# A graph-attention layer on one core: one product for K, V and Q rows, every gather from the K/V table, and gathers held closer to the compute

## The reference

```python
Q = x @ Wq + bq;  K = x @ Wk + bk;  V = x @ Wv + bv      # per node
E = edge_attr @ We + be                                  # per edge
score = (K[src] * Q[dst] / sqrt(12) * E).sum(-1)         # per edge and head
score = exp(clip(score, -5, 5))
wV = segment_sum(V[src] * score, dst);  Z = segment_sum(score, dst)
out = layernorm(x + wV / (Z + 1e-6))
```

## Time and profile before

| what | value |
|---|---|
| median of three runs | 1014.6 us |
| profiled execution, its span (the page shows no time around it) | 1301.3 us |
| POOL busy | 748.1 us (57%) |
| PE busy | 672.6 us (52%) |
| DVE busy | 653.2 us (50%) |
| ACT busy | 177.1 us (14%) |
| mean granted TensorE clock | 0.729 of full speed |

### The profile page before, as it was taken

How to read it: one execution, slowest core, us unless ns; L and a number is a source line. 1 busy time by engine, 2 the same in 40 slices (tenths; PEclk the granted TensorE clock), 3 DMA queues, 4 the chain that set the end, 5 groups by cost and what they waited for, 6 DMA issues and landing times.

```text
span 1301.3 us, 12054 instructions
## 1 busy us (share of the span) xinstructions
PE 672.6 (52%) x3352; PEld 461.0 (35%) x3352; DVE 653.2 (50%) x1307; ACT 177.1 (14%) x337; POOL 748.1 (57%) x788
## 2 busy tenths in 40 slices
PE   3834744755345464455564355545454565445343
PEld 3833422533223343333343233333333333333223
DVE  4311634864346554455554454555455555455446
ACT  1413101111011111011110111011011111111011
POOL 7172465265656665666666565666666666666640
PEclk8756866877677766767778676677767777677777
DMA  7643543544435444544545354544544445445420
GB/s 178 222 145 105 161 126 94 147 125 130 135 100 138 119 132 111 133 132 130 138 120 145 94 153 103 137 134 120 136 131 129 134 128 137 115 136 138 115 70 21
DMA packets 101206, 165.87 MB, mean 127 GB/s; under 512 B 45132, under 2 KB 63853, under 8 KB 101133
## 3 DMA queue, kind: packets, MB, share of 16 engines
q1 hardware_dynamic: 62829, 84.39, 23.4%
q0 software_dynamic: 37152, 75.74, 22.2%
q10 hardware_dynamic: 1152, 4.92, 0.9%
HBM read 152.57 MB, written 12.39 MB: 127 GB/s over the span
## 4 chain that ended last, share of the span: by engine, by line
another core or an unknown queue 40%; issue 22%; DVE 17%; PE 15%; ACT 4%; DMA 1%; DVEq 0%; SPq 0%
DVE qe L830 5%; PE psE L451 4%; DVE logit L919 4%; ACT qe L632 3%; PE psA L521 3%; PE psT L472 3%; DVE qke L910 2%; DVE clipped L925 1%; PE psQ L431 1%; DVE q_parts L809 1%; DVE ob L882 1%; PE psA L482 1%; DVE place L818 1%; DVE msg L937 1%
## 5 line engine op out<-in xcount | busy, mean ns | idle before, releaser
L390 POOL DMA_INDIRECT kv<-kv_table,idx x758 | 724.6, 956 | 514.3 <-issue 218.1
L521 PE MATMUL psA<-place,msg 128*104 128x104 f32 x1536 | 206.4, 301 | 339.7 <-DVE msg L937 253.5
L521 PEld LDWEIGHTS psA<-place,msg 128*104 128x104 f32 x1536 | 193.0, 212 | 369.9 <-DVE msg L937 270.5
L818 DVE TENSOR_TENSOR place<-psI,rel_tile 128x832 f32<-128x832 f32 (+1 forms) x99 | 98.6, 996 | 322.9 <-remote 322.9
L451 PE MATMUL psE<-ea,we 97*96 97x512 f32 x392 | 241.8, 750 | 0.8 <-ACT xt L613 0.8
L632 ACT ACTIVATE qe<-psE 96x1024 f32<-96x1024 f32 (+1 forms) x99 | 99.9, 1009 | 573.4 <-remote 432.5
L830 DVE TENSOR_TENSOR qe<-psQ,qe 96x1024 f32<-96x1024 f32 (+1 forms) x99 | 118.9, 1201 | 60.7 <-ACT qe L632 35.5
L472 PE MATMUL psT<-identity,qe 96*128 96x96 f32 x782 | 109.7, 297 | 74.5 <-DVE qe L830 56.2
L472 PEld LDWEIGHTS psT<-identity,qe 96*128 96x128 f32 x782 | 92.1, 174 | 88.9 <-DVE qe L830 63.8
L910 DVE TENSOR_TENSOR qke<-psT,kv 128x768 f32<-128x768 f32 (+1 forms) x99 | 92.9, 938 | 29.0 <-remote 25.1
L451 PEld LDWEIGHTS psE<-ea,we 97*96 97x96 f32 x392 | 71.5, 206 | 74.5 <-issue 73.5
(11 more groups left out here) (117 smaller groups left out, 405.6 us busy)
## 6 DMA issues: line engine op xcount, KB each, us to landing
ea<-eaT SPq DMA_DIRECT2D x99, 384.0 KB
q_parts<-rel_table SPq DMA_DIRECT2D x99, 252.0 KB
kv<-kv_table,idx POOLq DMA_INDIRECT x758
qwin<-q_table SPq DMA_DIRECT2D x198, 23.6 KB
xb<-xrows SPq DMA_DIRECT2D x24, 144.0 KB
out<-ob SPq DMA_DIRECT2D x24, 144.0 KB
q_table<-q_parts SPq DMA_DIRECT2D x4, 720.0 KB
kv_table<-kv ACTq DMA_DIRECT2D x2, 960.0 KB
```

The source lines that it names most:

```text
L390: pool.indirect_dma_start(kv[:, k, t], None, kv_table, sources).then_inc(kv_in[k], 16)
L521: last = nc.tensor.matmul(sums[0:ML, off:off + PW], msg[:, s, t], place[:, s, t], start=opens, stop=closes)
L818: nc.vector.tensor_tensor(place[:, k % 2, 0:nt], ps_ids.unsqueeze(1).broadcast_to([P, nt, PW]), rel_tile[:, bass.ds(g * T, nt)].unsqueeze( ...
```

## The change

The three groups that were gathered from the input go away, with their transposes, copies and products; all 99 groups gather from `kv_table`, and the first gather waits for `kv_out` and the whole of `idx`. K, V and Q rows come from one product of 288 columns; the banks are now three pairs (`node_banks`). ACT copies K and V to `kv_stage`, and Q, scaled, as float32 to a new tile `q_full` in SBUF. The split into parts reads `q_full`: ACT's leading parts are put between the copies, DVE's remainders are made in place (five of them ahead of the window tables, five behind), all ten middle parts come after all leading ones. `q_table` is stored in the eight chunks of `KV_CHUNKS`. The order of some loads on SP changes. `CLOSE` becomes 2, so the wait for `q_done` begins with group 2 instead of 16; and from group 2 on the second half of a group's gathers also waits for `t_done` of the group two back.

```diff
-CLOSE = 2 * U
+CLOSE = 2
-XG = 3
-Q_CHUNKS = (10, 10, 10, 10, 5, 5)
+EARLY_QUERIES = 5
-        xg = sb("xg", [P, XG, T, D], f32)
+        q_full = sb("q_full", [P, NR // P, D], f32)
-        kv_banks = [psE[:, 0], psE[:, 1], psA[:], psT[:, 0]]
+        node_banks = [psE, psQ, psT]
 # SP
-                        sp.dma_start(idx[:, 0:XG * T], src[:, 0:XG * T]).then_inc(idx_in, 16)
...
+                        sp.dma_start(idx[:], src).then_inc(idx_in, 16)
 # POOL
                         if first and at == 0:
                             pool.wait_ge(idx_in, 16)
-                        if first and at == XG:
-                            pool.wait_ge(idx_rest_in, 16)
                             pool.wait_ge(kv_out, 16 * len(KV_CHUNKS))
                         k = at % U
                         for t in range(tiles(at)):
+                            if first and at >= CLOSE and t == tiles(at) // 2:
+                                pool.wait_ge(t_done, at - 1)
                             sources = bass.IndirectOffsetOnAxis(ap=idx[:, at * T + t:at * T + t + 1], axis=0)
-                            if first and at < XG:
-                                pool.indirect_dma_start(xg[:, k, t], None, xrows, sources).then_inc(xg_in[k], 16)
-                            else:
-                                pool.indirect_dma_start(kv[:, k, t], None, kv_table, sources
-                                                        ).then_inc(kv_in[k], 16)
+                            pool.indirect_dma_start(kv[:, k, t], None, kv_table, sources).then_inc(kv_in[k], 16)
 # PE
-                                if n >= 4:
-                                    pe.wait_ge(kv_up, n - 3)
+                                if n >= 3:
+                                    pe.wait_ge(kv_up, n - 2)
+                                    pe.wait_ge(q_full_up, n - 2)
                                 for j in range(2):
-                                    last = nc.tensor.matmul(kv_banks[n % 4][:, j * 2 * D:(j + 1) * 2 * D],
-                                                            nodes[:, t + j], wn[:, 0:2 * D],
+                                    last = nc.tensor.matmul(node_banks[n % 3][:, j, 0:3 * D], nodes[:, t + j], wn[:],
                                                             start=True, stop=True)
-                        for tile, size in chunked(Q_CHUNKS):
...
-                        for n in range(2 * XG):
-                            pe.wait_ge(xg_in[n // 2], 16 * T)
...
-                        for g in range(XG):
-                            convert(g)
 # ACT
+                            nc.scalar.activation(kv_stage[:, 2 * n:2 * n + 2], node_banks[n % 3][:, :, 0:2 * D],
+                                                 ACT.Copy).then_inc(kv_up, 1)
+                            nc.scalar.activation(q_full[:, 2 * n:2 * n + 2], node_banks[n % 3][:, :, 2 * D:3 * D],
+                                                 ACT.Copy, scale=float(HD) ** -0.5).then_inc(q_full_up, 1)
                             if n in ends:
                                 store_nodes(n)
+                            if 2 * n >= QB * (split + 1):
+                                leading(split)
+                                split += 1
...
+                        for n in range(NR // P // QB):
+                            middle(n)
 # DVE
+                            nc.vector.tensor_tensor(q_full[:, n * QB:(n + 1) * QB], q_full[:, n * QB:(n + 1) * QB],
+                                                    q_parts[:, n * QB:(n + 1) * QB, 0], ALU.subtract).then_inc(q_r, 1)
```

More of the change, by code:

```diff
@@ L165, in gnn_program @@
         tables_chain, tables_up, rel_out = sem("tables_chain"), sem("tables_up"), sem("rel_out")
-        idx_in, idx_rest_in = sem("idx_in"), sem("idx_rest_in")
-        xg_in = [sem(f"xg_in{i}") for i in range(XG)]
-        turned, turned_up, conv_mm, conv_up = sem("turned"), sem("turned_up"), sem("conv_mm"), sem("conv_up")
+        idx_in = sem("idx_in")
         kv_in = [sem(f"kv_in{i}") for i in range(U)]
@@ L264, in _ @@
                         sp.wait_ge(xt_in[3], 16)
-                        load_nodes(5)
+                        for c in range(5, len(KV_CHUNKS)):
+                            load_nodes(c)
                         sp.wait_ge(range_up, 1)
@@ L282, in _ @@
                     if first:
-                        for c, (tile, size) in enumerate(chunked(Q_CHUNKS)):
+                        for c, (tile, size) in enumerate(chunked(KV_CHUNKS)):
                             if c == 0:
@@ L395, in _ @@
                     for s in range(U):
-                        groups = len(range(s, NG, U)) - (1 if first and s < XG else 0)
+                        groups = len(range(s, NG, U))
                         missing = (T - TAIL_TILES[s]) if s < len(TAIL_TILES) else 0
                         pool.wait_ge(kv_in[s], 16 * (T * groups - missing))
-                    if first:
-                        for s in range(XG):
-                            pool.wait_ge(xg_in[s], 16 * T)
                     nc.gpsimd.dma_reset()
@@ L415, in _ @@
                                 n = (tile + t) // 2
-                                if n >= 4:
-                                    pe.wait_ge(kv_up, n - 3)
+                                if n >= 3:
+                                    pe.wait_ge(kv_up, n - 2)
+                                    pe.wait_ge(q_full_up, n - 2)
                                 for j in range(2):
-                                    last = nc.tensor.matmul(kv_banks[n % 4][:, j * 2 * D:(j + 1) * 2 * D],
-                                                            nodes[:, t + j], wn[:, 0:2 * D],
+                                    last = nc.tensor.matmul(node_banks[n % 3][:, j, 0:3 * D], nodes[:, t + j], wn[:],
                                                             start=True, stop=True)
                                 last.then_inc(kv_mm, 1)
-                        pe.wait_ge(kv_up, NR // P // 2)
-                        for tile, size in chunked(Q_CHUNKS):
[L425 to L434, removed]
                         pe.wait_ge(we_in, 16)
                         pe.wait_ge(ones_set, 3)
-                        pe.wait_ge(q_r, NR // P // QB)
+                        pe.wait_ge(q_full_up, NR // P // 2)
                     def halves_of(at):
@@ L526, in _ @@
                         pe.wait_ge(ids_up, 2)
-                        for n in range(2 * XG):
-                            pe.wait_ge(xg_in[n // 2], 16 * T)
[L529 to L549, removed]
                     edge_rows(0, 0, 0)
-                    if first:
-                        for g in range(XG):
-                            convert(g)
                     query_rows(0, 0, 0)
-                    if first:
-                        pe.wait_ge(conv_up, T // 2 * XG)
                     to_rows(0, 0, 0)
@@ L581, in store_nodes, with leading, middle @@
                                 kv_stage[:, tile:tile + size]).then_inc(kv_out, 16)
+                        def leading(n):
+                            act.wait_ge(q_full_up, -(-QB * (n + 1) // 2))
+                            nc.scalar.activation(q_parts[:, n * QB:(n + 1) * QB, 0], q_full[:, n * QB:(n + 1) * QB],
+                                                 ACT.Copy).then_inc(q_hi, 1)
+                        def middle(n):
+                            act.wait_ge(q_r, n + 1)
+                            nc.scalar.activation(q_parts[:, n * QB:(n + 1) * QB, 1], q_full[:, n * QB:(n + 1) * QB],
+                                                 ACT.Copy).then_inc(q_mid, 1)
@@ L583, in _ @@
+                        split = 0
                         for n in range(NR // P // 2):
                             act.wait_ge(kv_mm, n + 1)
[L585 to L588, removed]
+                            nc.scalar.activation(kv_stage[:, 2 * n:2 * n + 2], node_banks[n % 3][:, :, 0:2 * D],
+                                                 ACT.Copy).then_inc(kv_up, 1)
+                            nc.scalar.activation(q_full[:, 2 * n:2 * n + 2], node_banks[n % 3][:, :, 2 * D:3 * D],
+                                                 ACT.Copy, scale=float(HD) ** -0.5).then_inc(q_full_up, 1)
@@ L610, in _ @@
-                    if first:
-                        for n in range(2 * XG):
-                            act.wait_ge(turned, n + 1)
-                            nc.scalar.activation(xt[0:D, n * 4 * P:(n + 1) * 4 * P], turn_banks[n % 4][0:D, :],
-                                                 ACT.Copy).then_inc(turned_up, 1)
+                        for n in range(split, NR // P // QB):
+                            leading(n)
+                        for n in range(NR // P // QB):
+                            middle(n)
@@ L655, in _ @@
                     edges_up(0, 0, 0)
-                    if first:
-                        act.wait_ge(kv_out, 16 * len(KV_CHUNKS))
```

(19 more changed lines are left out.)

44 lines of the change are left out of this document (7 added, 37 removed).

## The result

The changed kernel takes 1049.05 us (median of four runs, 1048.28 to 1050.42), the kernel before, timed beside it, 1015.25 us (1014.39 to 1017.43): a ratio of 1.0336, with a 95% interval of 1.032 to 1.0352. It is slower by 34 us. The forecast was 1052.6 us.

The account below looks back on a forecast made before the run. The prediction took POOL's chain of gathers, 1.25 us each, to bound the kernel. 1014.6 + 30.0 (lost lead) + 5 (later table) + 3 (query rows) = 1052.6 us, own range 1040 to 1070, widened to 1030 and 1078.

Parts of the forecast that it names:

- What bounds the kernel: Whole kernel: a chain of gathers on POOL, 1.25 us each, first table gather at 49.4 us, 18 us after the last.
- the stops: Halts of POOL, DVE and ACT about every two groups, some 12 us each, taken as belonging to the profiled execution only.
- half-group hold: Second half of a group's gathers waiting for `t_done`: covered at group 2 and, by 18 us, in the loop; costs nothing.
- The lead: Start of POOL: 24 gathers of the first three groups move behind the table, nothing hides them, +30.0 us.
- The table: Node phase: the 288-column product makes the K/V table later, +5 us, bounds -5 and +9.5.
- The query rows: Gathers from group 2 on wait for the first query rows: +3 us, bounds 0 and 11.
- DVE beside POOL: Early gathers lengthened by DVE's splits with both operands in SBUF: 0 to 5 us, taken as nothing.
- the rest of the node phase: Second product, transposes and conversions leave PE and ACT: nothing won, as POOL is still busy with its first eight groups.
- The stops are real: Rival: timed runs are also held every second group, so the change saves 29 us, giving 986 us; chance 0.09.
- The lead was partly wasted: Rival: POOL waits for first messages before its ninth group, losing some 5 us of lead: 1048 us; chance 0.08.
- The half-group hold binds: Rival: in the loop landing takes 18 us longer, POOL runs in step with PE, about 1150 us; chance 0.04.
- The lead is made up: Rival: the table comes 30 us earlier and the time stays as before; chance 0.04.

Follow-up runs that it names:

- e1: The kernel before, unchanged, profiled once more: 1015.02 us (one run), a span of 1013.3 us.
- e3: The changed kernel without the second half group's wait for `t_done`, the wait for query rows from group 2 on kept: 1050.16 us, ratio 1.0347.
- e5: The changed kernel, unchanged, timed once more in five rounds beside other variants: 1050.33 us, ratio 1.0353.
- e4: The kernel before with all groups gathered from the K/V table, both products and the old holds kept: 1044.85 us, ratio 1.0286.
- e6: The changed kernel with three groups gathered from the input again and without both holds, leaving the merged product alone: 1014.16 us, ratio 1.0009.
- e10: The changed kernel with every last part of the Q rows computed twice on DVE, once into an unread tile: 1048.63 us.
- e2: The changed kernel without the wait for `t_done` and with `CLOSE` back at 16: 1044.33 us, ratio 1.0285.
- e7: The kernel before with four groups gathered from the input instead of three (`XG` = 4): 1009.12 us, ratio 0.9951.
- e9: The changed kernel with four groups gathered from the input and without both holds, the merged product kept: 1006.08 us, ratio 0.9918.

## Why the prediction was right, step by step

**What bounds the kernel: right.** The chain on POOL, at 1.25 us a gather, sets the time before and after, and the stops belonged to one profiled execution. The first table gather of before was put at 49.4 us from the median; it is at 43.6 (e1), and the missing 6 us lie in the pace: 757 intervals at (995.27 - 43.56) / 757 = 1.257 us instead of 1.25 are 5.5 us. From the end of the last gather to the end of the span are 1013.3 - 996.2 = 17.1 us, where 18 had been taken.

**The sum, term by term,** by the two profiles without stops. The last gather starts at 1030.03 instead of 995.27, 34.8 us later:

| term | predicted | measured | from |
|---|---|---|---|
| 24 gathers more behind the table | +30.0 | +30.1 | 24 x 1.255 |
| the table later | +5 | -3.3 | 40.24 - 43.56 |
| up to the 17th gather | +3 | +9.8 | 70.11 - 40.24 - 16 x 1.255 |
| half-group hold | 0 | 0 | e3 against e5 |
| pace of the other gathers | 0 | -1.8 | 757 x (1.2548 - 1.2572) |

*The lead: right,* and it is 29 of the 34 us by the times too (e4).

*The table: wrong in its sign.* Two parts of the step failed. The first is the price of 96 more columns. At the faster of two paces, a pair of tiles of the changed kernel starts 0.97 us after the one before it (x4 is one pair):

```profile
28.73 1.13 PE L404 MATMUL psE<-wn,xt 97*128 97x288 f32 x4
29.70 1.13 PE L404 MATMUL psQ<-wn,xt 97*128 97x288 f32 x4
```

In e1 (x8 is two pairs) it is 0.92 us on the mean of the 17 pairs from 18.98 us on:

```profile
30.93 1.94 PE L419 MATMUL psE<-wn,xt 97*128 97x192 f32 x8
32.70 1.10 PE L419 MATMUL psA<-wn,xt 97*128 97x192 f32 x4
33.64 1.10 PE L419 MATMUL psT<-wn,xt 97*128 97x192 f32 x4
34.57 0.81 PE L419 MATMUL psE<-wn,xt 97*128 97x192 f32 x4
```

The granted clock is 1.00 in both stretches. So 96 columns more cost 0.05 us a pair there, not 0.19; what else sets the length of a pair, no run separates. The first few pairs of both runs go at a slower pace, and between 192 and 288 columns the price there is larger than the 0.38 us taken: 1.28 us a pair in e1, 1.92 in the changed kernel. The step had set a bank of the earlier trace rows against a pair of the earlier trace rows as if only columns differed.

The second part is "the chain runs over PE". The last K/V store is issued at 36.4 us in the changed kernel and at 36.0 in e1, so PE and ACT are done no earlier; but it lands 3.0 us after its issue instead of 6.9. The end of the table is set by the stores' way through DMA, which the step had only as its lower bound, -5 from the x rows' traffic. Without the lead e4 has -2.8 and the changed kernel -3.3; e6, with the lead back, has +0.3.

*The query rows: the mechanism right, its size too small.* They are there 30 us after the table, near the upper end of 31 and far from the 11 without a queue. From the last split (48.2 us) to the first window load are 15.4 us, where 5.5 had been taken from the earlier trace rows. For 11.4 of them SP waits for the stores of `q_table`. By the pages of the changed kernel and of e1, a store of 720 KB takes 9.5 us to land instead of 4.5 (what, number, size, us to landing), as the changed kernel issues its eight stores within 6 us and e1 its six over 17:

```profile
q_table<-q_parts SPq DMA_DIRECT2D x2, 720.0 KB, 9.5
...
q_table<-q_parts SPq DMA_DIRECT2D x4, 720.0 KB, 4.5
```

By the window below the DMA engines of the changed kernel are full meanwhile, at 0.91 of their time and 316 GB/s.

```profile
40.20:62.20 22.00, 3.70 (x4) 0.96 (x4) 8.03 (x15) 3.90 (x6) 17.39 (x16) 0.58 0.91 316
```

That the stores and not the splits set this time, e10 shows. The 5.5 us had been taken from a stretch without a gather, in which the DMA engines were busy for 0.35 of their time (115.40 to 120.90 us in the trace of before). Of the 9.8 us, 7.6 are the wait beyond the usual issue time and 2.2 the slower gathers ahead of it. Without the holds, 7 us are saved by the times (e2), less than 9.8, as the slow gathers stay.

*DVE beside POOL: in its bounds, hidden.* Five gathers took 1.25 to 1.56 us instead of 0.95, all beside splits, and e10 makes it eight: within 0 to 5 us, and covered by the wait. The traces show a hold until the split at hand is over: a gather that begins beside a single split ends 0.82 us after that split, at 66.60 after 65.78 in the earlier trace rows and at 54.84 after 54.02 in e1:

```profile
53.60 1.24 POOL L390 DMA_INDIRECT kv<-kv_table,idx  x1 [0.30 <-issue]
```

Beside splits that follow one another every 0.57 us, the gathers start 1.71 us apart, three splits, and each ended after 1.40 us, so POOL is not held until the row of DVE's steps is over. The Trainium skill ("SBUF — State Buffer", on the "DVE blocks DMA" trap) has GpSimd unable to write descriptors while certain DVE operations run, with an fp32 copy as its example. The traces agree with such a hold to the end of one operation, here for a subtract of two operands in SBUF.

*The half-group hold and the rest of the node phase: right,* zero each (e3, e6).

So +5 + 3 = +8 stood where -3.3 + 9.8 - 1.8 = +4.7 was measured; the -1.8 us of the pace no run explains. Two wrong sizes of opposite sign left 3.6 us between the forecast and the time; that it is so little is luck, and the 30 us are owed to the chain.

**The rivals.** *The stops are real:* fell with e1. *The lead was partly wasted:* fell for the kernel before, where POOL's waits for messages are 1.2 us in all, four times the usual issue time; with a lead of four it is real (e7, 5.4 us). *The half-group hold binds:* fell with e3. *The lead is made up:* the table would have had to come 30 us earlier; it came 3.3.

**What would show it.** "First gather between 45 and 65 us" was wrong: 40.2, by the sign of the table's term. 782 gathers at 1.25 us, the wait ahead of the 17th gather (number 16 from zero) that ends with the first query rows, and no long wait for `to_rows` came as said.

What caused the stops stays open. Two profiled executions of one kernel have spans of 1301.3 and 1013.3 us, and no run tells what released the engines in the first.

## What to carry to other kernels

Where one queue issues at a steady pace and never rests, a change is priced by when that queue starts and what it waits for, and work taken from other engines is worth nothing until the queue waits for it (e6 against e9). A hold on such a queue costs what is missing between its place in the queue and the event, so the same line cost 7 us in one kernel and 37 in another. Set a suspicious profile against the median of the timed runs before anything is built on its waits.

## What the runs showed of the hardware that was not expected

- A profiled execution was 288 us longer than another of the same kernel, with stops every two groups, while the timed runs differ by 3 us.
- At a granted clock of 1.00, a pair of float32 tiles took 0.97 us with 288 columns and 0.92 with 192; among the first pairs of the product, where the granted clock also reads 1.00, it took 1.92 and 1.28.
- A gather of 128 rows that began beside a single DVE step on two operands in SBUF (128x480, 0.65 us) ended 0.82 us after the step (e1). Beside a row of such steps it takes 1.40 us instead of 0.95, and its issue time of 0.30 us stays.
- With the DMA engines busy for 0.88 of their time in both runs, a store of 720 KB took 9.5 us to land where eight stores were issued within 6 us, and 4.5 where six were spread over 17 (e1).
